# A gated cross-attention and expert block on one core: statistics in two places, x loaded first, and sums and normalisations at both ends of the attention in SBUF

## The reference

```python
def _layernorm(x): return (x - mean(x)) / sqrt(var(x) + 1e-5)        # over the 512 columns

# attention: 16 heads of 32, causal, q from the normalised x, k and v from the context
q, k, v = ln(x) @ Wq.T, ctx @ Wk.T, ctx @ Wv.T
probs   = softmax(where(causal, q k^T * 32**-0.5, -inf))
x       = x + tanh(g_xattn) * ((probs @ v) @ Wo.T + bo)

# experts: 8 of width 256, the best 6 of each row weighted by the router, and a shared one of width 512
h = ln(x)
y = sum over the 6 picked e of share_e * (silu(h @ wg_e) * (h @ wu_e)) @ wd_e
x = x + tanh(g_ffn) * (y + (silu(h @ wsg) * (h @ wsu)) @ wsd)
```

## Time and profile before

| what | value |
|---|---|
| runs | 1853.76 us median (1851.68 to 1855.23) |
| the profiled execution | 1855.56 us, its span 1852.9 us |
| busy, share of the span | PE 96%, VectorE 75%, ScalarE 52%, GpSimd 49% |
| granted TensorE clock, mean | 0.988 |
| chain that ended last | PE 66%, DVE 13%, POOL 7%, issue 6%, DMA 4% |
| instructions | 33849 |

### The profile page before, as it was taken

One profiled execution on the slowest core, in us unless ns is written; L12 is line 12 of the kernel. 1 busy time (PEld: TensorE's weight loads), 2 busy tenths in 40 slices (PEclk: granted clock), 3 DMA queues, 4 the chain that ended last, 5 costly groups with the idle time before them and its releaser, 6 DMA issues.

```text
span 1852.9 us, 33849 instructions
## 1 busy us (share of the span) xinstructions
PE 1784.4 (96%) x11904; PEld 1492.8 (81%) x11904; DVE 1392.1 (75%) x3117; ACT 961.8 (52%) x2260; POOL 912.9 (49%) x1185
## 2 busy tenths in 40 slices
PE   6899999999996999999999999999999999999999
PEld 5888888888885788888778878878888887888887
DVE  5677777777777877777977777788777778777776
ACT  4888788888887433433433333444333444333431
POOL 3677777777767443444533434543343462333330
PEclk8999999999997999999999999999999999999999
DMA  4778778987897312211142121123212113211111
GB/s 153 130 151 165 151 163 166 183 165 165 165 188 150 125 56 80 69 57 46 46 136 81 45 80 46 58 68 114 80 52 74 46 57 117 77 46 57 46 47 46
DMA packets 301000, 182.84 MB, mean 99 GB/s; under 512 B 210080, under 2 KB 265376, under 8 KB 300832
## 3 DMA queue, kind: packets, MB, share of 16 engines
q1 hardware_dynamic: 300832, 180.69, 40.0%
HBM read 111.43 MB, written 18.87 MB: 70 GB/s over the span
## 4 chain that ended last, share of the span: by engine, by line
PE 66%; DVE 13%; POOL 7%; issue 6%; DMA 4%; ACT 3%; SPq 1%; POOLq 0%; DVEq 0%; ACTq 0%
PE gate_up L1308 31%; PE down L1825 18%; PE bank L802 10%; PE scores L911 2%; DVE ops_lo L1165 2%; DVE acc L1676 2%; POOL halves L495 2%; POOL hidden L1524 1%; DMA c_in<-in_ctx_t 1%; PE rows_t L792 1%; DVE probs L732 1%; ACT probs L605 1%; DMA x_res<-in_x 1%; PE y_values L933 1%; DVE xo_lo L1110 1%
## 5 line engine op out<-in xcount | busy, mean ns | idle before, releaser
L1308 PE MATMUL gate_up<-xo_hi,ops_hi 128*128 128x512 f32 x1120 | 440.0, 393 | 14.1 <-DVE gated L1284 5.2
L1308 PE MATMUL gate_up<-xo_lo,ops_hi 128*128 128x512 f32 x1120 | 436.1, 389 | 0.0
L1308 PE MATMUL gate_up<-xo_hi,ops_lo 128*128 128x512 f32 x1120 | 436.0, 389 | 0.0
L495 POOL TENSOR_TENSOR halves<-probs,halves 128x384 f16<-128x384 f32 x244 | 223.1, 928 | 84.8 <-ACT halves L599 84.0
L1308 PEld LDWEIGHTS gate_up<-xo_hi,ops_hi 128*128 128x128 f32 x1120 | 210.2, 188 | 67.6 <-DVE gated L1284 10.5
L1676 DVE SCALAR_TENSOR_TENSOR acc<-down,scale,acc 128x512 f32<-128x512 f32 x320 | 238.1, 745 | 34.8 <-PE down L1825 34.3
L1524 POOL TENSOR_TENSOR hidden<-hidden,gated 128x512 f32<-128x512 f32 x120 | 157.2, 1317 | 190.1 <-DVE hidden L1289 170.5
L1825 PE MATMUL down<-d_hi,h_hi 128*128 128x512 f32 x640 | 249.1, 389 | 0.0
L1825 PE MATMUL down<-d_lo,h_hi 128*128 128x512 f32 x640 | 249.0, 389 | 0.0
L1825 PE MATMUL down<-d_hi,h_lo 128*128 128x512 f32 x640 | 249.0, 389 | 0.0
L1308 PEld LDWEIGHTS gate_up<-xo_lo,ops_hi 128*128 128x128 f32 x1120 | 210.2, 188 | 43.9
(11 more groups left out here) (189 smaller groups left out, 4213.2 us busy)
## 6 DMA issues: line engine op xcount, KB each, us to landing
g_raw<-in_w_gate SPq DMA_DIRECT2D x40, 512.0 KB, 3.6
u_raw<-in_w_up SPq DMA_DIRECT2D x40, 512.0 KB, 3.6
d_raw<-in_w_down SPq DMA_DIRECT2D x40, 512.0 KB, 3.4
c_in<-in_ctx_t SPq DMA_DIRECT2D x16, 512.0 KB, 4.4
x_res<-in_x SPq DMA_DIRECT2D x16, 512.0 KB, 5.8
x_between<-x_res SPq DMA_DIRECT2D x16, 512.0 KB, 3.4
acc<-x_between SPq DMA_DIRECT2D x32, 256.0 KB, 4.7
out<-acc SPq DMA_DIRECT2D x32, 256.0 KB, 3.3
```

Source lines behind the costliest of these rows:

```text
L495: pool.tensor_tensor(halves[k % HALVES][:, 1, :], probs[k % RING][:], halves[k % HALVES][:, 0, :], ALU.subtract).then_inc(p_lo_made, 1)
L1308: ins = pe.matmul(gu_ps[bank][:], ops[x][:, which, a, c, :], xo[y][:, b, c, :], start=(begins and c == 0 and i == 0), stop=(c == CH - 1 an ...
```

## The change

It has five parts.

1. **Statistics in two places.** The two `bn_stats` stay in slot 5 (`row_statistics`); the chain behind them moves to slot 7 of iterations 0 and later (`GUESS_SLOT`), and with it GpSimd's Newton iteration from slot 7 to 8.
2. **x loaded first.** The load of x moves from slot 1 to slot 0, ahead of the store of the result.
3. **Sums of y in SBUF** for groups 0 and 1 of batch 0, groups 2 and 3 of batch 14 and all of batch 15 (`sums_in_sbuf`); the scores no longer wait for those groups.
4. **The first normalisations in SBUF.** Batches 0, 1 and 2 are normalised by `tensor_scalar` with both scalars from SBUF; the scores of batches 0 and 1 don't wait for them. Batch 2's moves from slot 13 to 14, behind `close_group`.
5. **x_t's loads over two iterations**: slots 5 and 9 of iteration 13 and 4 and 7 of iteration 14. The first up weights are loaded in slot 6 of iteration 15 and not right behind the gate weights.

```diff
+    Y_PSUM, Y_SBUF = 2 * JH, H * (B - 2) + 2 * JH
-    X_T_LOADS = (1, 4, 6, 8)
-    X_LOAD, RES_LOAD, C_LOAD, GATE_LOAD, ROWS_LOAD = 1, 2, 9, 12, 13
-    LN_SLOT, NEWTON_SLOT, XN_SLOT = 5, 7, 13
+    X_T_LOADS = ((-1, 5), (-1, 9), (0, 4), (0, 7))
+    UP_LOAD = 6
+    X_LOAD, RES_LOAD, C_LOAD, GATE_LOAD, ROWS_LOAD = 0, 2, 9, 12, 13
+    LN_SLOT, GUESS_SLOT, NEWTON_SLOT, XN_SLOT = 5, 7, 8, 13
+    XN_PSUM = 3
-    FIRST_XN_SLOT, BIAS_SLOT = 3, 10
+    FIRST_XN_SLOT, SECOND_XN_SLOT, BIAS_SLOT = 3, 14, 10
-    def is_tail(b, g):
-        return b.k == B - 1 and g >= H // JH - 2
+    def sums_in_sbuf(b, g):
+        return head(b, JH * g) >= Y_SBUF or head(b, JH * g) < Y_PSUM
+    def two_before(i, g):
+        return (i + -1, g + 1) if g < H // JH - 1 else (i, 0)
...
                         turn(head(*bh))
+                    if s == X_LOAD and has(i, 2):
+                        wait(sp, xt_done, ln.times(T, -T))
+                        sp.dma_start(x_of(ln)[:], row(x_v, ln)).then_inc(x_loaded[ln.k % 2], DMA)
                     if s == (2 if is_end(i) else 0) and has(i, -2):
...
-                    if s in X_T_LOADS and phase(i) == 0:
-                        start.sync(sp, phase(i), X_T_LOADS.index(s))
+                    if (phase(i), s) in X_T_LOADS:
+                        start.sync(sp, 0, X_T_LOADS.index((phase(i), s)))
+                    if s == UP_LOAD and phase(i) == 1:
+                        start.sync(sp, phase(i), 0)
...
-            def statistics(ln):
+            def row_statistics(ln):
                 dve.wait_ge(x_loaded[ln.k % 2], DMA * (ln.k // 2 + 1))
                 for t in range(T):
                     dve.bn_stats(stats[:, t, :], x_of(ln)[:, t, :]).then_inc(norm_chain, 1)
+            def statistics(ln):
                 dve.wait_ge(norm_chain, ln.times(NORM_STEPS, T))
...
             def normalise(ln):
                 dve.wait_ge(rstd_made, ln.times(1, 1))
+                if ln.k < XN_PSUM:
+                    for t in range(T):
+                        dve.tensor_scalar(x_of(ln)[:, t, :], x_of(ln)[:, t, :], mv[:, t, 0:1], rstd[:, t:t + 1],
+                                          ALU.subtract, ALU.mult).then_inc(xn_made, 1)
+                    return
...
-                whole = y_sum[:].rearrange("p (t h) d -> p t h d", t=T) if is_tail(b, g) else y_sum_ps
+                whole = y_sum[:].rearrange("p (t h) d -> p t h d", t=T) if sums_in_sbuf(b, g) else y_sum_ps
...
                     if s == places(i).moments and has(i, 2):
+                        row_statistics(ln)
+                    if s == (GUESS_SLOT if i.k >= 0 else places(i).moments) and has(i, 2):
                         statistics(ln)
...
-                    if s == places(i).normal and has(i, 2):
+                    if s == (places(i).normal if i.k else SECOND_XN_SLOT) and has(i, 2):
                         normalise(ln)
...
-                if g == 0 and has(i, 1):
+                if g == 0 and has(i, 1) and i.k + 1 >= XN_PSUM:
                     pe.wait_ge(xn_made, i.times(T, 2 * T))
-                wait(pe, y_made, i.times(H // JH, g - H // JH + 2))
+                if not sums_in_sbuf(*two_before(i, g)):
+                    wait(pe, y_made, i.times(H // JH, g - H // JH + 2))
```

More of the change, by code:

```diff
@@ L442, in run @@
                         rows_again(hat_tile(i + 1))
-                    if s == X_LOAD and has(i, 2):
-                        wait(sp, xt_done, ln.times(T, -T))
-                        sp.dma_start(x_of(ln)[:], row(x_v, ln)).then_inc(x_loaded[ln.k % 2], DMA)
                     if s == 3 and phase(i) == 2:
@@ L647, in normalise @@
                 dve.wait_ge(rstd_made, ln.times(1, 1))
+                if ln.k < XN_PSUM:
[3 more added lines that the diff above has]
+                    return
                 wait(dve, xn_made, ln.times(T))
                 dve.tensor_copy(rstd_ps, rstd[:]).then_inc(rstd_kept, 1)
-                dve.wait_ge(rstd_kept, ln.times(1, 1))
+                dve.wait_ge(rstd_kept, ln.times(1, 1 - XN_PSUM))
                 for t in range(T):
@@ L662, in vector @@
             weights_lo(1)
+            row_statistics(At(0, 2, 0))
             statistics(At(0, 2, 0))
@@ L1375, in start_sync @@
             load_raw(sp, GATE, 0)
+        elif (phase, part) == (1, 0):
             load_raw(sp, UP, 0)
```

## The result

The changed kernel takes 1841.29 us (median of 4 runs, 1840.45 to 1843.02), the kernel before 1854.49 beside it. The ratio is 0.9928, 95% interval 0.9909 to 0.9947: 13.2 us faster, where 17.2 were forecast. The profiled execution took 1841.56 us, its span went from 1852.9 to 1839.6 us.

A forecast was written before the change was run, and what follows sets the result against it. TensorE was taken to set the end nearly everywhere, its attention waits being mostly scores waiting for y. Opening 5.0, middle 9.5 and end 2.7 sum to 17.2 us, off the median of 1853.76: 1836.5 us, range 1831 to 1842.

The forecast's parts named there:

- the middle: Middle iterations: statistics split and x loaded early gain 9.5 us, as 6.0 + 2.7 + 0.8; bounds 5 and 11.
- The opening: Iterations 0 and 1: sums and normalisations in SBUF remove two TensorE waits, gaining 5.0 us; bounds 2.4 and 7.2.
- the first wait: Opening, TensorE's 5.05 us wait at 39.26 us: 2.4 us passes on, through ScalarE getting ahead.
- The second wait: Opening, TensorE's 4.81 us wait at 71.26 us: 3.4 us gained, less 0.8 for a lock with GpSimd, so 2.6.
- half of a sign of being wrong: Opening: VectorE's normalisations take over 1 us each and ScalarE starts batch 1 no earlier.
- The 1838.7: Opening: time in us if product and normalisation each lose up to 2.4 us to GpSimd by the port rule.
- The ten short waits: Middle: ten TensorE waits for y of 0.20 to 0.27 us, 2.1 us in all, of which 0.8 was counted.
- One sign of being wrong: Middle: a period above 33.7 us in iterations 8 to 10.
- the one on SyncE's queue: Store behind x's load: x_res's wait may grow by up to 3.3 us, turns behind it; priced at 0.
- The end: End of the attention: ScalarE's 1.99 us wait and a 0.73 us turned-tile wait go, gaining 2.7; bounds 0 and 5.06.
- The moved steps cost what the late waits did: Rival, VectorE's slot 7: 1.6 us lost in each of 13 iterations, 1858.1 us, slower by 4.3; chance 0.06.
- Both ends give little: Rival: other engines set the pace there, so the opening gives 2.4 and the end 0; 1841.8 us; chance 0.14.

The follow-up runs named there:

- The split alone: The kernel before with one edit: the statistics' small steps go to slot 7 and the Newton iteration to slot 8; 1841.5 us, ratio 0.9935.

## Why the prediction was right, and the step that failed

The time of 1841.3 fell inside the range of 1831 to 1842, close to its upper end, and partly by luck: in the two profiled executions 1.3 to 1.7 us of the lead are the clock's, and the middle brought less than half of its 9.5.

**The opening: 3.2 us by its edits, for 5.0.** Of the lead of 5.5 at iteration 2, the kernel with the opening undone has 2.3 as well. 1.7 of these are there at the first group of scores (37.57 against 39.26) and come from no edited step. The changed kernel shows the same: batch 0's second transposes start at 23.72 us, no earlier than before (23.50), but VectorE's first remainder of v at 27.77 where it was 29.11. TensorE's clock makes that (last section). The split leads by 0.6 at iteration 2 when it stands alone. Against the kernel with the opening undone, which had the full clock from 20 to 30 us too, the first wait gave 3.3 us, where 2.4 were counted. ScalarE's high part of the transposes came without its wait of 1.93 us, as forecast, and 2.2 us earlier (40.62 for 42.79). The second wait gave 3.25 us (2.6 counted), and 2.9 to 3.1 of them were given back at the next group, so that next to nothing of this term was left. There TensorE waits for GpSimd, whose context low part was not late enough to show before:

```profile
59.99 1.57 POOL L515 TENSOR_SCALAR bias<-bias,tanh_gates 128x512 f32<-128x512 f32 x1
...
64.50 2.54 POOL L496 TENSOR_TENSOR c_lo<-c_in,c_hi 128x1024 fp32r<-128x1024 f32 x1
64.75 3.63 DVE L662 TENSOR_SCALAR x_odd<-x_odd,mv,rstd 128x512 f32<-128x512 f32 x2
...
67.09 0.58 PE L822 MATMUL bank<-c_hi,w_hi 128*128 128x256 f32 x1 [3.20 <-POOL c_lo L496]
```

The two normalisations of batch 0 took 1.00 us together, 0.5 each for the 0.45 taken; those of batch 1, at the first wait, took 1.81 beside a GpSimd instruction of 1.16, more than the 1.41 before, and those of batch 2, above, 3.63 beside GpSimd's 2.54, over 1 us each, which is half of a sign of being wrong; the other half, a ScalarE that starts batch 1 no earlier, did not come. The rule of the Trainium skill weighed in the prediction (SBUF — State Buffer, section "Who interferes with whom") is borne out by these rows and by the small steps of 0.17 and 1.21 us above. The 1838.7 that went by it missed for the same reason as the forecast; how its 2.2 us follow from losses of up to 2.4 is not worked out there.

**The middle: the split's price right, one cost left out.** In the two kernels without the early load the middle gave 8.9 and 9.3 us, for 9.5. Iteration 4 gave 3.6 + 2.2 for 6.0, iterations 7 and 11 3.8 for 2.7. The ten short waits gave 0.27 each and took 0.34 back at the fourth group, through the lock in slot 7; 0.8 was counted, about -0.7 came. So the sum is right partly because two errors offset, and the early load, which the prediction counted into the 6.0, had no part in it. That the small steps meet x_res was forecast; that slack in the slots behind hides it was not quite so. One sign of being wrong came with it, by a hair: iterations 8 to 10 take 33.73 to 33.79 us each, before 33.67 to 33.69.

The step that failed is the one on SyncE's queue: "the turns of heads 1 and on behind it. These wait for GpSimd anyway [...]: I take 0." It looked at the turns behind the load of x_res. The turn that counts is that of head 15, which used to stand between store and load and now has both ahead of it. In iterations 3 to 13 of the changed kernel it lands 5.1 to 7.4 us after its issue, before 3.6 to 4.8 us. In iteration 8 it lands 6.5 us after its issue at 309.31, so at 315.8, and the last group's values, its own the last of four, start at 315.65: TensorE runs on the heels of that transfer.

Set instruction by instruction beside the kernel with the load behind the store, the changed one loses 5.0 us between iterations 2 and 14, in two places. 2.2 are lost at head 15's values in iterations 3, 4, 12 and 13, which start 0.04 or 0.05 us after the turn has landed. 2.7 are lost in iterations 5, 7 and 11 to 13 in the projection of v, where TensorE waits for q_lo, late by the lock of slot 7. One of each:

```profile
180.47 0.20 PE L952 MATMUL y_values<-v_parts,turned 128*128 128x64 bf16 x1 [0.54 <-DMA turned<-halves]
292.88 0.51 PE L822 MATMUL bank<-w_hi,c_hi 128*128 128x512 f32 x1 [0.91 <-DVE q_lo L770]
```

That the early load brings the second is not shown: with the opening undone x is first too, and iteration 7 goes without that wait. But while x is first, taking it away gains nothing. With x_res in slot 9 it is gone, and head 15's values wait that much longer. The four kernels with x first and the statistics split start iteration 14 at 508.9, 509.5, 509.7 and 509.9 us, whichever other part is changed. With the load behind the store, an earlier opening and a later x_res each move that start, by 5.6 and 2.5 us. I take the pace of that queue for the reason that only 1.6 us of waits for turned tiles are listed, and that the opening's gain and that of a later x_res pass on so badly.

The early load took 4.6 to 5 us from the middle (4.3 for 8.9 to 9.3; 3.4 by the medians), 8.2 where x_res is in slot 9 (4.3 for 12.5), and 9.8 us from the kernel before without the split. What lets the split version issue that turn earlier against its use than the unsplit one is not settled: in iteration 8 TensorE gets to head 15's values 7.1 us after the issue, against 5.9 in the kernel before with x first, and 5.7 in the changed one with the statistics in one place.

The Trainium skill (DMA: Bandwidth & Descriptors, section "Two DMAs through the same engine are not ordered") says that descriptors of one queue start in order. The turn's 3.7 us behind 512 KB and 6.4 to 7.1 behind 1 MB, in iteration 8, agree.

**The end: 3.5 for 2.7.** At iteration 14's fourth group 0.9 came (0.73 forecast), at iteration 15's second 4.8, of which 2.2 were given back, since TensorE then waits for the products, for turned tiles and for maxima:

```profile
550.78 0.24 PE L952 MATMUL y_values<-v_parts,turned 128*128 128x64 bf16 x1 [3.79 <-DVE y L708]
...
553.19 0.23 PE L952 MATMUL y_values<-v_parts,turned 128*128 128x64 bf16 x1 [1.02 <-DMA turned<-halves]
555.32 0.80 PE L932 MATMUL scores<-k_hi,q_hi 32*128 32x128 f32 x8 [1.55 <-DVE neg_max L750]
```

The split alone, without the end's edits, gains 0.4 there, so about 3 us are theirs.

**The rivals.** "The moved steps cost what the late waits did" fell: with the store first they cost 0.3 us in an iteration. "Both ends give little" gave the right time, 1841.8, for the wrong reason: the opening's edits did give little, but the end gave 3.5, and most of what is missing is the middle's. The early load did land earlier, in iteration 4 at 176.8 us for 186.5; what it displaced was the price.

**How far the numbers go.** The table of starts is of one execution each. Executions of one kernel differ by 2 to 10 us, and the 23 of the kernel before by 11.5. The intervals of the ratios are some 5 to 7 us wide in all but the largest sets, so that two experiments 2 or 3 us apart are told apart by their traces and not by their times. The split alone was profiled in its longest of five (1844.8, median 1841.5). Terms of 1 us are sure where many traces repeat them, as the 0.3 per iteration, and not as differences of medians.

## What to carry to other kernels

When a transfer moves forward in a queue, list every transfer that it now stands ahead of, with the deadline of each, those of the iteration before among them; the victim here was one small transpose whose turn came between two large ones. Time each part of a combined change alone: here one part was worth as much as the whole, and another took back a good part of that. And where a freed wait brings less than its length, look for the engine that TensorE now follows without a listed wait.

## What the runs showed of the hardware

The same standstill left the clock alone or not. Before the second transposes of the opening TensorE waits 2.09 us in both kernels. The clock and what TensorE got done in the 10 us around and behind it, of the kernel before, the one with the load in slot 0 and the store in 1 (edited in SyncE's queue alone), and the changed one:

```profile
20.00:30.00 10.00, 7.91 (x38) 0.83 0.41 142
```

```profile
20.00:30.00 10.00, 7.91 (x51) 1.00 0.44 148
```

```profile
20.00:30.00 10.00, 7.91 (x51) 1.00 0.47 152
```

In the first the clock falls to the lower of its levels, 1.2 GHz, for part of the stretch, and 1.3 to 1.7 us are lost by VectorE's first remainder of v (29.11 us for 27.77 and 27.43). It fell in six of the fourteen profiled executions: in two of the eight with the new opening, and in four of the six with the old one. So 1.3 to 1.7 of the 13.3 us between the two profiled executions may belong to the execution and not to the change.
